# First task's operands picked on chip, and a separate bank for late projections, in an attention and mixture-of-experts layer

## The reference

```python
mod = (silu(c) @ wmod).reshape(2, 6, 1, 128)            # shift, scale, gate, twice
h = layernorm(x) * (1 + ca) + sa                        # x is (2, 1024, 128)
Q = (h @ W_dq) @ W_uq;  K = (h @ W_dkv) @ W_uk;  V = (h @ W_dkv) @ W_uv
x = x + ga * (softmax(causal(Q @ K.T / sqrt(8))) @ V) @ W_o      # 16 heads of 8
h = layernorm(x) * (1 + cb) + sb
logits = relu(h @ Wr1 + br1) @ Wr2 + br2                # 8 experts, the best two of each token
x = x + gb * (shared_ffn(h) + sum of w_e * expert_e(h)) # silu, hidden width 512
```

## Time and profile before

| | us |
|---|---|
| runs | 455.4, 458.18, 458.71 (median 458.18) |
| the profiled execution | 457.29 |
| its span, first to last instruction | 455.5 |
| TensorE busy | 415.4 (91%) |
| VectorE busy | 320.2 (70%) |
| ScalarE busy | 266.0 (58%) |
| GpSimd busy | 140.6 (31%) |
| mean granted clock | 0.953 |

### The profile page before, as it was taken

One profiled execution on the slowest core, in us unless ns is written; L12 is line 12 of the kernel. 1 busy time (PEld: TensorE's weight loads), 2 busy tenths in 40 slices (PEclk: granted clock), 3 DMA queues, 4 the chain that ended last, 5 costly groups with the idle time before them and its releaser, 6 DMA issues.

```text
span 455.5 us, 9376 instructions
## 1 busy us (share of the span) xinstructions
PE 415.4 (91%) x2926; PEld 238.1 (52%) x2926; DVE 320.2 (70%) x1192; ACT 266.0 (58%) x609; POOL 140.6 (31%) x236
## 2 busy tenths in 40 slices
PE   7688799999999999999998999999679779999983
PEld 3343323443534534544534434347567559999953
DVE  5669868897988888898977886256755335555637
ACT  3536636656767576757665667867346254455652
POOL 2241700010010200127483325041762743333530
PEclk9979958999999999999999999999959959999999
DMA  5254051033030300400400001950121223210135
GB/s 146 62 147 130 12 155 53 1 106 141 13 96 1 88 21 0 108 1 1 108 18 12 21 26 38 324 123 12 49 58 31 76 59 82 66 42 26 36 103 199
DMA packets 28796, 31.78 MB, mean 70 GB/s; under 512 B 4827, under 2 KB 23363, under 8 KB 28243
## 3 DMA queue, kind: packets, MB, share of 16 engines
q1 hardware_dynamic: 25959, 25.82, 20.1%
q0 software_dynamic: 2272, 4.67, 3.0%
q10 hardware_dynamic: 516, 0.69, 0.5%
HBM read 21.04 MB, written 9.85 MB: 68 GB/s over the span
## 4 chain that ended last, share of the span: by engine, by line
PE 76%; DVE 8%; another core or an unknown queue 4%; DMA 3%; ACT 3%; issue 3%; POOL 2%; SPq 0%; DVEq 0%; ACTq 0%; POOLq 0%
PE oacc L1710 14%; PE mx L1657 14%; PE sc L1688 13%; PE sc L1843 7%; PE oacc L1858 7%; PE sc L1693 3%; PE mx L1810 2%; PE mx L1799 2%; PE mx L1719 2%; DVE mxp L1271 1%; PE sc L1799 1%; POOL parts L629 1%; PE mx L1580 1%; DMA parts<-token_results 1%
## 5 line engine op out<-in xcount | busy, mean ns | idle before, releaser
L911 ACT ACTIVATE pr<-sc 128x512 f32<-128x512 f32 (+1 forms) x296 | 155.1, 578 | 88.0 <-PE sc L1693 43.5
L1657 PE MATMUL mx<-S 72*128 72x512 bf16 (+3 forms) x384 | 115.3, 340 | 10.6 <-DMA S<-k_parts 4.4
L1267 DVE CUSTOM_DVE_ANT_0 masked<-mx,later 128x128 f32<-128x128 f32 (+3 forms) x256 | 111.3, 486 | 16.3 <-PE mx L1657 15.3
L1688 PE MATMUL sc<-S 75*128 75x512 bf16 (+3 forms) x374 | 110.5, 332 | 0.0
L1271 DVE TENSOR_REDUCE mxp<-mx 128x1 f32<-128x512 f32 x128 | 81.4, 684 | 22.1 <-PE mx L1657 21.8
L1710 PE MATMUL oacc<-pr,vb 128*32 128x512 f32 (+3 forms) x768 | 75.7, 503 | 0.0
L975 ACT ACTIVATE pr<-sc,bcur 128x128 f32<-128x128 f32 x156 | 44.5, 369 | 34.6 <-PE sc L1843 18.6
L1657 PEld LDWEIGHTS mx<-S 72*128 72x128 bf16 x384 | 34.0, 100 | 56.7 <-DVE mxp L1271 21.8
L1688 PEld LDWEIGHTS sc<-S 75*128 75x128 bf16 x374 | 35.4, 99 | 46.9 <-issue 22.8
L756 POOL DMA_INDIRECT token_results<-S,xrow x39 | 38.4, 983 | 65.1 <-DVE S L1408 63.1
L1858 PEld LDWEIGHTS oacc<-vb,pr 128*128 128x128 f32 x312 | 41.3, 202 | 13.5 <-issue 13.0
(11 more groups left out here) (291 smaller groups left out, 481.2 us busy)
## 6 DMA issues: line engine op xcount, KB each, us to landing
S<-k_parts SPq DMA_DIRECT2D x21, 192.0 KB
S<-q_parts SPq DMA_DIRECT2D x42, 96.0 KB
xrow<-slot_rows SPq DMA_DIRECT2D x39, 64.5 KB, 1.8
S<-in_we SPq DMA_DIRECT2D x1, 2048.0 KB, 9.7
S<-in_we SPq DMA_DIRECT2D x4, 512.0 KB, 10.3
parts<-token_results SPq DMA_DIRECT2D x4, 512.0 KB, 5.3
x_sb<-in_x SPq DMA_DIRECT2D x4, 256.0 KB, 3.9
out_y<-attn SPq DMA_DIRECT2D x4, 256.0 KB, 2.3
```

The source lines that it names most:

```text
L911: act.activation(pr[:, group % NBUF, h:h + n, at:at + w], src, ACT.Exp, scale=float(DK) ** -0.5).then_inc(s["exp_done"], 1)
L1267: ins = dve.tensor_tensor_reduce(masked[:, d % 2, w * m:w * m + w], unit[a][:, w * m:w * m + w], later[:, HALF - w:HALF], 1.0, LOWEST, ALU ...
L1657: ins = pe.matmul(dst[:, w * m:w * m + w], S3[0:CROSS, r3, 1, q:q + P], S3[0:CROSS, r3, 0, kk:kk + w], start=(m == 0), stop=True, skip_gro ...
L1688: ins = pe.matmul(dst[:, w * m:w * m + w], S3[0:CROSS + 3, r3, 0, kk:kk + P], S3[0:CROSS + 3, r3, 1, q:q + w], start=(m == 0), stop=True, ...
```

## The change

It concerns the first task's first half of positions, and the places of batch 0's values and batch 1's projections and values.

- **Picking.** GpSimd builds `picks`, matrices of zeros and ones of 32 by 72. TensorE multiplies the three parts of Q and K (first half, 32 rows) by them, 24 products of 512 columns in four groups (`pick_rows`), which sum in PSUM to the 72 rows of two heads each; ScalarE copies each group (72 by 1024) into `S3` (`rows_out`). The stores and loads of that half are gone. The second half still goes through memory, Q first, and the waits for it are on `first_q` (unit 11) and `first_k` (unit 15).
- **Order of the front.** Batch 0's second half is projected Q first and gets other banks. The square root for batch 1 moves behind the copies and the middle parts, VectorE's fourth residue moves ahead of the rstd, GpSimd's three low parts move behind its memsets. Sixteen products with 64 or 24 rows stand ahead of the first maximum. ScalarE takes an exponential of one column behind the normalisations.
- **A bank of their own.** Batch 0's values leave the front and stand in the list behind maximum units 3 and 7. All `proj` and `val` units use `oacc`'s second bank instead of the ring; its first weighing waits for the last of them.
- **Splitting.** The steps of a late projection follow at once, with `mid` and `low` of each at the place of the next one. `h_out` of batch 1 stands at the place of its turning in the list.
- **List.** `MAXES_AFTER` is spread out and ends 41 units ahead instead of 38; `FILL_AFTER` adds one and two products behind scores 9 and 10.

The core of the diff:

```diff
-MAXES_AFTER = [2] * 9 + [4] * 2 + [2] * 3
+MAXES_AFTER = [2] * 4 + [3] * 4 + [2] * 2 + [1] * 5 + [2 if g % 4 == 0 else 1 for g in range(28)]
+FILL_AFTER = {9: 1, 10: 2}
 FILLERS = {(0, k): 2 if k < 3 else 1 for k in (0, 1, 2, 3, 4, 5, 7, 8, 10)}
 SPLIT = 5
 LAG = 3
 OUT = 3
 LAST_LAG = 4
-BETWEEN = {(0, 6): [("xturn", 2, 0)], (0, 9): [("xturn", 3, 0)], (0, 11): [("proj", 4, 0)], (0, 14): [("proj", 5, 0)],
+BETWEEN = {(0, 3): [("val", 0, 0)], (0, 7): [("val", 1, 0)], (0, 6): [("xturn", 2, 0)], (0, 9): [("xturn", 3, 0)], (0, 11): [("proj", 4, 0)], (0, 14): [("proj", 5, 0)],
...
+ON_ACT = {("proj", 4, 0), ("proj", 5, 0), ("proj", 6, 0), ("proj", 7, 0), *(("val", g, 0) for g in range(4)), ("at", 0, 0), ("at", 1, 0), ("at", 3, 0), ("at", 3, 1), ("x2t", 0, 0), ("x2t", 1, 0), ("x2t", 3, 0), ("x2t", 3, 1), ("rt", 0, 0), ("rt", 1, 0), ("rt", 3, 0), ("rt", 3, 1), *UPS}
...
+        elif kind in ("proj", "val"):
+            b = 5
...
-        QK = [(b, kq, half) for b in range(B) for half in range(2) for kq in range(2)]
-        qk_bank = [bank[2], oacc[:, 0, :], oacc[:, 1, :]]
+        QK = [(0, 0, 0), (0, 1, 0), (0, 1, 1), (0, 0, 1)] + [(1, kq, half) for half in range(2) for kq in range(2)]
+        qk_bank = [bank[2], oacc[:, 0, :], mx[:, 2, :], bank[2]]
+        picks = pr[0:HQ * DK, 0, :, :].rearrange("p h n -> p (h n)").bitcast(BF16)[:, 0:2 * 3 * HQ * CROSS].rearrange(
+            "p (s a h r) -> p s a h r", s=2, a=3, h=HQ)
+        rows_bank = [mx[:, 0:2, :], oacc[:, 0:2, :], sc[:, 0:2, :], mx[:, 0:2, :]]
...
-            def store_first(half):
-
-                cols = slice(HALF * half, HALF * half + HALF)
+            def store_first():
+
+                cols = slice(HALF, S)
                 for part in range(3):
-                    for kq in range(2):
-                        sp.wait_ge(*part_done(part, QK.index((0, kq, half))))
-                        dst = q0[half, part] if kq else kd[0, 0, :, part, :, cols]
-                        sp.dma_start(dst, parts[0:HQ * DK, kq, part, cols]).then_inc(s[("k_out", f"q_out{half}")[kq]], 16)
+                    for kq in (1, 0):
+                        sp.wait_ge(*part_done(part, QK.index((0, kq, 1))))
+                        dst = q0[part] if kq else kd[0, 0, :, part, :, cols]
+                        sp.dma_start(dst, parts[0:HQ * DK, kq, part, cols]).then_inc(s[("k_out", "q_out")[kq]], 16)
+
+            def load_first():
+
+                sp.wait_ge(s["q_out"], 48)
+                sp.dma_start(S3[0:CROSS, 1, 1, QW:2 * QW],
+                             q0.rearrange("a d h n -> (a d) (h n)").unsqueeze(1).broadcast_to([3 * DK, 3, QW])
+                             ).then_inc(s["first_q"], 16)
+                sp.wait_ge(s["k_out"], 48)
+                load_k(0, slice(HALF, S), s["first_k"])
...
+            store_first()
+            load_first()
...
+            chained(pool.memset(picks[:, :, :, :, :].rearrange("p s a h r -> p (s a h r)"), 0.0))
+            unit_of = identb[0:HQ * DK, 0:HQ * DK].rearrange("p (d h) -> p h d", h=HQ)
+            for part in range(3):
+                pool.tensor_copy(picks[:, 0, part, :, :].rearrange("p h (r d a) -> p h r d a", r=3, a=3)[:, :, :, :, part],
+                                 unit_of.unsqueeze(2).broadcast_to([HQ * DK, HQ, 3, DK])).then_inc(s["sel_ready"], 1)
+                pool.tensor_copy(picks[:, 1, part, :, 3 * DK * part:3 * DK * part + 3 * DK].rearrange("p h (d r) -> p h d r", r=3),
+                                 unit_of.unsqueeze(3).broadcast_to([HQ * DK, HQ, DK, 3])).then_inc(s["sel_ready"], 1)
...
-            for n in (0, 2, 3):
-                low(n, r1[:, n % 2, :])
...
+            for n in (0, 2, 3):
+                low(n, r1[:, n % 2, :])
...
+                pool.wait_ge(*freed(("val", 2 * b + 1, 0)))
...
-                    split.append((t, 0))
+                    residue(t)
+                    if t > 4:
+                        low(t - 1, raw[(t - 1) % 4])
+                elif kind == "val" and t == 2:
+                    low(7, raw[3])
...
+            def rows_out(n):
+
+                kq, h = n % 2, n // 2 * 2
+                act.wait_ge(s["rows_ready"], n + 1)
+                dst = (S3[0:CROSS, 1, 0, :].rearrange("r (h n) -> r h n", h=HQ)[:, h:h + 2, 0:HALF],
+                       S3[0:CROSS, 1, 1, 0:QW].rearrange("r (h n) -> r h n", h=HQ)[:, h:h + 2, :])[kq]
+                act.activation(dst, rows_bank[n][0:CROSS], ACT.Copy).then_inc(s["rows_out"], 1)
...
+            rows_out(0)
+            rows_out(1)
             hi(2)
-            root(2)
             hi(3)
-            load_first_q(act, 0)
+            rows_out(2)
+            rows_out(3)
             mid(2)
             mid(3)
-            v_out(0)
-            v_out(1)
+            root(2)
...
-            h_out(2)
-            h_out(3)
+            act.activation(turned[:, 0:1], ident[:, 0:1], ACT.Exp)
...
+                elif kind == "xturn":
+                    h_out(t)
                 elif kind == "proj":
                     raw_out(t, PLACE[kind, t, k])
-                    split.append((t, 0))
+                    hi(t)
+                    if t > 4:
+                        mid(t - 1)
                 elif kind == "val":
                     value_out(t, PLACE[kind, t, k])
+                    if t == 2:
+                        mid(7)
...
             residue(2)
+            residue(3)
             rstd(STATS[2], (s["std_ready"], 3))
             dve.scalar_tensor_tensor(out=shift[:, STATS[2]], in0=mv[:, STATS[2], 0], scalar=-1.0, in1=rst[:, STATS[2]],
                                      op0=ALU.mult, op1=ALU.mult).then_inc(s["shift_ready"], 1)
-            residue(3)
...
-            warm(3)
+
+            def pick_rows(n, parts_of):
+
+                kq, h = n % 2, n // 2 * 2
+                for part in parts_of:
+                    for m in range(2):
+                        ins = pe.matmul(rows_bank[n][0:CROSS, m, :], picks[:, kq, part, h + m, :],
+                                        parts[0:HQ * DK, kq, part, 0:HALF], start=(part == 0), stop=(part == 2))
+                return ins
+
+            pe.wait_ge(s["sel_ready"], 6)
+            pe.wait_ge(s["hi_ready"], 1)
+            pick_rows(0, [0])
+            pe.wait_ge(s["mid_ready"], 1)
+            pick_rows(0, [1])
+            pe.wait_ge(s["hi_ready"], 2)
+            pe.wait_ge(s["r1_ready"], 2)
+            pick_rows(1, [0])
+            pe.wait_ge(s["mid_ready"], 2)
+            pick_rows(1, [1])
+            pe.wait_ge(*low_done(0))
+            pick_rows(0, [2]).then_inc(s["rows_ready"], 1)
+            pe.wait_ge(*low_done(1))
+            pick_rows(1, [2]).then_inc(s["rows_ready"], 1)
             project(2)
             project(3)
-            for g in range(2):
-                values_to(bank[g], g).then_inc(s["v_ready"], 1)
+            pick_rows(2, range(3)).then_inc(s["rows_ready"], 1)
+            pe.wait_ge(s["rows_out"], 1)
+            pick_rows(3, range(3)).then_inc(s["rows_ready"], 1)
+            pe.wait_ge(s["rows_out"], 3)
+            for _ in range(4):
+                for g in range(2):
+                    pe.matmul(oacc[:, g, :], identb[64 * g:64 * g + 64, :],
+                              after[64 * g:64 * g + 64, :, :].rearrange("p h n -> p (h n)"), start=True, stop=True)
+            for _ in range(2):
+                for g in range(4):
+                    pe.matmul((oacc[:, 0, :], oacc[:, 1, :], sc[:, 0, :], sc[:, 1, :])[g], identb[32 * g:32 * g + 24, :],
+                              after[32 * g:32 * g + 24, :, :].rearrange("p h n -> p (h n)"), start=True, stop=True)
...
-                if t == 0 and k in (0, LAST_MAX[0] + 1):
-                    pe.wait_ge(s[f"first_in{c}"], 16 * 4)
+                if t == 0 and k == 0:
+                    pe.wait_ge(s["rows_out"], 4)
+                if t == 0 and k == LAST_MAX[0] + 1:
+                    pe.wait_ge(s["first_q"], 16)
+                if t == 0 and c and diagonal:
+                    pe.wait_ge(s["first_k"], 48)
...
+                elif j == 0 and c == 1:
+                    pe.wait_ge(*freed(("val", 3, 0)))
...
+                    if NU * t + k in FILL_AFTER:
+                        pe.wait_ge(*freed(("val", 3, 0)))
+                        fill(oacc[:, 1, :], FILL_AFTER[NU * t + k])
```

More of the change, by code:

```diff
@@ L105 @@
 VALUES_AT = 13
-HI_AT, RES_AT, MID_AT, LOW_AT = 2, 3, 6, 7
 def attention_order(tasks):
@@ L261, in adaln_layer @@
         bank = [sc[:, 0, :], sc[:, 1, :], sc[:, 2, :], mx[:, 0, :]]
-        unit = [(mx[:, 0, :], mx[:, 1, :], mx[:, 2, :], sc[:, 2, :], oacc[:, 0, :])[b] for b in HELD]
+        unit = [(mx[:, 0, :], mx[:, 1, :], mx[:, 2, :], sc[:, 2, :], oacc[:, 0, :], oacc[:, 1, :])[b] for b in HELD]
         x_sb = sb("x_sb", [P, NT, C], F32)
@@ L435, in low_done @@
             return (s["lo1_ready"], 1) if n == 1 else (s["lo_ready"], max(n, 1))
-        def load_first_q(queue, c):
-            queue.wait_ge(s[f"q_out{c}"], 48)
```

(24 more changed lines are left out.)

24 lines of the change are left out of this document (7 added, 17 removed).

## The result

The changed kernel took 462.54 us, median of 4 runs (460.40 to 464.71), against 458.22, median of 4 (455.40 to 458.71), for the kernel before: a ratio of 1.0095, interval 1.0049 to 1.0141. Forecast was 451.0, with a range of 447.0 to 456.5. The profiled execution took 460.40 us, its span 458.7 against 455.5. Chips differ (the kernel before takes 457 to 458 us on two of those used here and 442 to 443 on others), so times are compared by their ratio to the kernel before on the same chip. Runs more than 1.5% above the fastest of their kernel are left out of its ratio: one of four in e5, two of four in e6 and in e8, one of ten in e3 and two of ten in e12.

What follows compares the result with a forecast made beforehand. TensorE was taken as the bound, losing time where it idles or runs at half clock. 2.2 + 5.2 - 0.65 = 6.75, less 0.45 gives 6.3: 457.3 - 6.3 = 451.0 us, range 447 to 456.5.

Steps and rivals of the forecast that it cites:

- 0.45 us taken off for handovers: In the sum: 0.45 us subtracted from the 6.75 us gain for handovers laid edge to edge.
- Part 5: From S0.11 (task 0's score unit 11) on: full clock stays, 5.2 us gained; 0.65 owed; longer lead priced 0.
- Those three (0.65 us of TensorE) are owed afterwards: -0.65: Behind S0.18: three maxima fewer come before that score, so their 0.65 us of TensorE is paid later.
- Part 1: Front to the first maximum: product ready 1.3 us sooner, but VectorE's first maximum 0.4 us later, at 25.5.
- so both are free: Front: building zero/one matrices on idle GpSimd and moving its memsets before the low parts cost nothing.
- They also bridge the gap that cost the clock: Front: the 16 warm-up products before the first maximum fill the TensorE gap behind the clock's first fall.
- The step that a gain is expected and none comes: Front: the product comes 1.3 us sooner, but VectorE's rstd waits for the later square root, so no gain.
- Part 2: Maxima up to the first score: S0.0 stays at 39.7, gain 0, bounds 1 us sooner to 1.5 later.
- Part 3 and 4: S0.0 to task 0's last maximum, 2.0 us sooner; then to S0.11, 2.2 us sooner including that 2.0.
- the rival: First rival: the clock falls again before S0.11, leaving only 2.2 - 0.65, so 455.8 us; chance 0.18 with its kin.
- Slower: Rival: clock falls in the front, in VectorE's late start, and again before S0.11: +2.25, so 459.5 us; chance 0.06.

Runs made afterwards that it cites:

- e5: The changed kernel as it is, run again on another chip as the yardstick: 1.0110 of the kernel before.
- e6: The kernel before with three extra maxima in its list, so 41 ahead, nothing else changed: 1.0198 of the kernel before.
- e8: The changed kernel with 38 maxima ahead, zeroing of `vb` behind the low parts, square root right behind the third high part: 0.9803 of the kernel before, by two runs.
- e3: The changed kernel with batch 1's square root right behind the third high part: 1.0086 of the kernel before.
- e12: The changed kernel with GpSimd's rows for the experts three scores later, 41 maxima still ahead: 1.0036 of the kernel before.
- e11: The changed kernel with the kernel before's list of maxima (38 ahead, old spread): 0.9892 of the kernel before.
- e1: The changed kernel with 38 maxima ahead instead of 41, its new spread over the first scores kept: 0.9891 of the kernel before.
- e9: e8 with four more filling products behind scores 7 to 9 of task 0: 0.9840 of the kernel before.
- e7: The changed kernel with the late modulation and the gates' product three maximum units later in the list: 1.0085 of the kernel before.

## Why the prediction was wrong

**The gain came, and was lost behind it.** At S0.18 the forecast had 7.4 us in hand (2.2 and 5.2) and 6.5 came (65.19 against 71.71). (The 0.45 us taken off for handovers rests on no row.) The step that failed is the last of Part 5: "In the long run the list runs 41 instead of 38 maxima ahead: three more, again 0.65, given back at the end of the attention, where fewer remain; 0, with 0.65 as its bad end." It was priced at 0; from W0.8 to W7.11 the kernel after takes 9.9 us more than the one before. In the changed kernel with 38 ahead that is 0.0 (e11) and 1.2 (e1); in the kernel before with 41 ahead, e6, it is 7.7, so it is neither the separate bank nor the front. With that one term mended the changed kernel is at 0.989 (e1, e11), near the forecast's 0.986. The maxima ahead were priced by TensorE's time for them. What they do is shift two kinds of work against each other: work hung on maximum units (the gates, the split of the negated maxima) comes three units earlier against work hung on scores (normalisations, weighings), and each engine takes the list in order. It was said at the start that TensorE is the bound behind 71 us, so what comes sooner is kept. That holds only while the order keeps every wait covered. Of the measured time itself, 2.6 us came back in the expert stage by a shorter stretch at half clock, which nobody forecast: that part is luck.

**"Those three (0.65 us of TensorE) are owed afterwards: -0.65"** was priced on the wrong engine as well. From W0.4 to W0.8 the new list has 20 maximum units where the old one has 16, and 2.0 us were lost there. e1 has 19 and takes 13.4 us, e11 16 and 11.4: 0.65 a unit, which is VectorE's 0.61 to 0.65 and not TensorE's 0.215.

**Part 1.** "so both are free" failed: the zeroing runs beside L1086 and costs 1.65 us of VectorE (2.7 in the six other profiles), and the low parts run beside rstd and cost 1.1. Forecast 25.5, measured 27.26. "They also bridge the gap that cost the clock" failed too in this profile: the clock was at half from 22.9 to 26.3, through the warm-ups, and the first product came at 25.30 where 23.0 was forecast. The step that a gain is expected and none comes, for the root's place, held: e9, with the root early and the zeroing late, gains it. The picks (0.22 us each) and the four copies (1.02 each; 1.04 taken) were right. The warm-ups of 64 rows took 1.71 for eight, at half clock; at full clock, in e9, 1.04.

**Part 2.** Forecast 0, S0.0 at 39.7, with 1.5 as the late bound. It started at 41.14, 1.4 late, just inside: the late front went through VectorE, which ended M0.10 at 35.96 (forecast 34.1), and the second lot of values started at 32.66 (forecast 30.75). The first exponential came only 0.5 later than before, since the table load was out of its way. The load took 1.28 us and the next ACTIVATE started 0.02 behind it, at 31.83, as the row said.

**Part 3 and 4.** The last maximum of task 0 ended at 52.93, forecast 51.9, before 53.9; half of the 2.0 us. The turned maxima were copied out at 55.80 (before 57.04) and S0.11 started at 58.46 (forecast 57.7, before 59.91): 1.45 of 2.2.

**Part 5, the clock.** Right: TensorE busy 2.95 of 3.5 us before 57.5, no fall, S0.11 to W0.4 in 5.73 us instead of 10.39, and S0.11 to S0.18 in 6.73 where 6.6 was forecast. That one execution of e8 fell at 52.3 in nearly this order shows that the rival was a near one; whether e9's fillers keep it away or chance does, six runs don't settle.

**The rivals.** Slower came, and not by the mechanism named. Its first half was seen, half clock in the front; its second, the fall before S0.11, was not. The rival on that side was sought in the front, where the change works, though the new list was in the diff and reaches to the end of the attention. e6 shows that this one line costs 2.0% in a kernel that has nothing else of the change.

What stays open: how the 6.1 us of W4.4 to W5.8 divide. Read from the traces are 1.6 (the wait for GpSimd's fourth normalisation), 1.6 (the meeting, by which the wait got shorter in e12) and 1.5 (the sixteen products at half clock, 3.44 us instead of 1.92); 1.4 is not assigned. That these add up was not tested: no run removed all of them with 41 ahead, and none moved the split of the maxima behind the fourth normalisation.

## What to carry to other kernels

Where one list orders all engines, a change of how far one kind of work runs ahead is not paid in that work's own time: go along the whole list and look for work that is hung on the other kind, and at what stands behind it in each engine's queue. When an idle engine is given something, look at what its neighbour does in the same microseconds: for GpSimd and VectorE the price in these rows was the whole rest of the other's instruction. And run the smallest line of a diff by itself: here it held more than the loss.

## What the runs showed of the hardware

- VectorE beside GpSimd: four normalisations of 128x128 took 1.12 us alone, 2.77 and 2.49 beside GpSimd's zeroing, and 3.83 to 3.86 in six profiles where its copy of 0.26 us took 1.44 beside them as well; an instruction of 0.17 us took up to 1.02, ending with GpSimd's to within 0.1 us. Masked maxima out of PSUM kept their pitch of 0.21 us.
- The clock fell at 22.9 in the kernel after although TensorE was busy all of 14 to 22.9 us; its last pause was 8.2 to 9.4. In e7 and e11, whose front is the same, it stayed whole there, and in e1 and e12 it fell at 24.4 and 24.3. No run says why.
- The eight warm-up products of 64 rows take 0.13 us each at full clock in e9 (1.04 for eight), where 512 columns of 72 rows take 0.22: so products on the two halves of the rows overlapped.
